# The second norm's blocks turned by VectorE behind a trip through DRAM, instead of by TensorE

## The reference

```
mod = silu(c) @ wmod            # sa, ca, ga, sb, cb, gb
h = layernorm(x) * (1 + ca) + sa
x = x + ga * (h @ (weight * blockmask).T + bias)        # 1024 x 1024, mask by 32 x 32 blocks
h = layernorm(x) * (1 + cb) + sb
x = x + gb * ((silu(h @ gate_w.T * gate_s) * (h @ up_w.T * up_s)) @ down_w.T * down_s)   # 2752 wide
```

## Time and profile before

| | us |
|---|---|
| median of 3 runs (lowest, highest) | 1110.01 (1108.84, 1110.47) |
| profiled execution | 1110.46 |
| its span, first to last instruction | 1108.7 |
| TensorE busy | 1080.1 |
| VectorE busy | 739.0 |
| ScalarE busy | 428.1 |
| GpSimd busy | 376.4 |

### The profile page before, as it was taken

The page is one execution under the profiler, slowest core; times in us unless marked ns, Lnnn a source line. Parts: engine busy times, 40 slices in busy tenths (PEclk is TensorE's granted clock), DMA queues, the critical chain, the costliest instruction groups (busy, mean ns, idle before and its releaser), DMA issues. The chain is left out here.

```text
span 1108.7 us, 13305 instructions
## 1 busy us (share of the span) xinstructions
PE 1080.1 (97%) x4753; PEld 501.3 (45%) x4753; DVE 739.0 (67%) x939; ACT 428.1 (39%) x783; POOL 376.4 (34%) x348
## 2 busy tenths in 40 slices
PE   5999999999999999999999999999999999999998
PEld 3443444545444444444444444444444444444444
DVE  4448478766688998889797888879545434334434
ACT  2322157556564554446555555555432000000000
POOL 2115446647644442326455555655200000000000
PEclk9999999999999999999999999999999999999999
DMA  9994223235453655445666666665298666566430
GB/s 345 388 388 114 80 72 95 68 103 162 143 194 129 169 174 171 129 125 166 195 205 180 184 191 184 186 203 180 74 353 330 246 251 235 223 240 235 194 127 38
DMA packets 132049, 206.94 MB, mean 187 GB/s; under 512 B 20624, under 2 KB 99216, under 8 KB 129552
## 3 DMA queue, kind: packets, MB, share of 16 engines
q1 hardware_dynamic: 126688, 184.08, 50.4%
q0 software_dynamic: 5296, 22.02, 5.6%
HBM read 137.39 MB, written 68.68 MB: 186 GB/s over the span
## 5 line engine op out<-in xcount | busy, mean ns | idle before, releaser
L1436 PE MATMUL pA<-work 128*128 128x512 f16 x1680 | 377.0, 379 | 5.1 <-ACT work L1097 3.3
L1436 PEld LDWEIGHTS pA<-work 128*128 128x128 f16 x1680 | 163.8, 98 | 205.4 <-ACT work L1097 6.4
L1236 PE MATMUL pA<-work 128*128 128x512 f32 x512 | 227.3, 595 | 2.5 <-DVE work L1696 0.9
L1436 PE MATMUL pB<-work 128*128 128x512 f16 x752 | 175.9, 379 | 1.4 <-DVE work L1855 1.4
L1236 PEld LDWEIGHTS pA<-work 128*128 128x128 f32 x512 | 94.3, 190 | 112.9 <-issue 109.9
L1877 DVE SCALAR_TENSOR_TENSOR work<-work 128x512 f16<-128x512 f16 x144 | 122.7, 874 | 19.6 <-ACT work L1117 19.3
L1503 PE MATMUL pA<-work 128*128 128x512 f16 x600 | 134.4, 379 | 0.0
L1097 ACT ACTIVATE work<-pA 128x512 f32<-128x512 f32 x126 | 74.6, 592 | 116.3 <-PE pA L1436 111.0
L1436 PEld LDWEIGHTS pB<-work 128*128 128x128 f16 x752 | 73.5, 98 | 90.2 <-DVE work L1855 2.1
L946 ACT ACTIVATE work<-pB,small 128x128 f32<-128x128 f32 x240 | 86.8, 478 | 70.6 <-PE pB L1209 59.3
L1503 PE MATMUL pB<-work 128*128 128x512 f16 x480 | 107.5, 379 | 0.9 <-DMA work<-h_left_scratch 0.9
(11 more groups left out here) (178 smaller groups left out, 1058.9 us busy)
## 6 DMA issues: line engine op xcount, KB each, us to landing
work<-h_scratch SPq DMA_DIRECT2D x8, 4480.0 KB, 13.7
h_scratch<-work SPq DMA_DIRECT2D x60, 512.0 KB, 3.1
work<-in_L_wmod SPq DMA_DIRECT2D x10, 2048.0 KB, 16.6
work<-in_L_ffn_gate_w SPq DMA_DIRECT2D x84, 128.0 KB, 3.2
work<-in_L_ffn_up_w SPq DMA_DIRECT2D x84, 128.0 KB, 2.9
work<-down_scratch SPq DMA_DIRECT2D x7, 1280.0 KB, 11.5
work<-in_L_ffn_down_w SPq DMA_DIRECT2D x68, 128.0 KB, 2.8
work<-in_L_attn_data SPq DMA_DIRECT2D x16, 512.0 KB, 4.2
```

The source lines that it names most:

```text
L1236: last = pe.matmul(pA[:, 2 * par(t) + h, :], hT1[par(t)][:, c, :], wT[:, c, h * H:(h + 1) * H], start=(c == 0), stop=(c == KT - 1))
L1436: last = pe.matmul(ps, w[:, m, c], bc[b][:, mv_, s, c], start=begin, stop=(i == n - 1 and c == KT // 2 - 1 and s == 1), skip_group_check=True)
```

## The change

The second norm's blocks are no longer turned by TensorE. `normalise(1, t)` writes `z2` in its own order of columns, SyncE stores it to a scratch in DRAM (`store_z`) and loads it back in four loads arranged like those of the weights (`load_zb`) into `zb`, which shares its place with a row used before and after. VectorE then turns it in one instruction into `z2T` in PSUM (`turn`), from where ScalarE goes on as before. There is one `zb`: `load_zb(t)` waits for the store of block t and for `turn(t - 1)`; `normalise(1, t)` waits for the store of block t-1.

The lists change with it. In VectorE's step t the first norm of block t+2 comes directly behind its statistics, ahead of the `lo_part`s; `turn` stands at the step's start (tables `FIRST` and steps 10 on) or behind `residual` (`SECOND`). The first two residuals are taken apart into scaling and finishing, and the second norm of block 0 goes behind `residual(2)`. On TensorE `gate_row(2)` stands ahead of the products of block 2 and the row sums 4 and 5 one place earlier, with `copy_row(5)` ahead of `evacuate(1)` on ScalarE. A mask quarter has one counter for its two loads in place of two. A wait of GpSimd for its own earlier root is added. The core of the diff:

```
+    z_v = z_d.rearrange("n (b j) (a k) -> n a j b k", b=A, a=A)
-        m_loaded = [sem(f"m_loaded{k}") for k in range(8)]
+        m_loaded = [sem(f"m_loaded{q}") for q in range(4)]
-        MID = {3: 0, 6: 1, 7: 3, 8: 5, 9: 6, **{t: t - 2 for t in range(10, NT + 1)}}
-        END = {6: 2, 7: 4, 9: 7}
+        zb = gbs
+        FIRST = {6: 1, 7: 3, 8: 5, 9: 6}
+        SECOND = {6: 2, 7: 4, 9: 7}
...
+            def store_z(t):
+                sp.wait_ge(z_done[1], t + 1)
+                sp.dma_start(z_d[t], z2).then_inc(z_stored, 16)
+            def load_zb(t):
+                sp.wait_ge(z_stored, 16 * (t + 1))
+                if t == 0:
+                    sp.wait_ge(acc_used, 2)
+                else:
+                    sp.wait_ge(t_done[1], t)
+                for a in range(A):
+                    sp.dma_start(zb[Q * a:Q * (a + 1)].rearrange("p (b k) -> p b k", b=A), z_v[t, a])\
+                      .then_inc(zb_loaded, 16)
...
+                if t in (3, 4):
+                    store_z(t - 3)
+                if t == 4:
+                    load_zb(0)
+                if t == 5:
+                    store_z(2)
+                    load_zb(1)
+                if t in FIRST:
+                    store_z(FIRST[t] + 2)
+                    load_zb(FIRST[t] + 1)
+                if t >= 10:
+                    store_z(t - 1)
+                    load_zb(t - 1)
+                if t in SECOND:
+                    if t < 9:
+                        store_z(SECOND[t] + 2)
+                    load_zb(SECOND[t] + 1)
...
+            row_sum(4)
             attend(1, 1, range(4, 6))
-            row_sum(4)
+            row_sum(5)
             attend(1, 1, range(6, KT))
-            row_sum(5)
+            gate_row(2, rowp[0])
...
-                if t in MID:
-                    transpose(1, MID[t])
-                if t in END:
-                    transpose(1, END[t])
-                if g == 1:
-                    transpose(1, LAST)
...
+            def turn(t):
+                dve.wait_ge(zb_loaded, 16 * A * (t + 1))
                 if t >= 1:
+                    dve.wait_ge(hf_ready, t)
+                else:
+                    dve.wait_ge(row_copied, 10)
+                dst = z2T.rearrange("p h n -> p (h n)")
+                dve.transpose(dst.rearrange("p (c b i) -> p c b i", c=KT, b=A),
+                              zb.rearrange("p (b c i) -> p c b i", b=A, c=KT)).then_inc(t_done[1], 1)
...
             def mask_quarter(q):
                 g, half = quarter(4 * q)
+                dve.wait_ge(m_loaded[q], 32)
                 for i in range(2):
-                    dve.wait_ge(m_loaded[2 * q + i], 16)
...
             for t in range(6, NT + 1):
+                if t in FIRST:
+                    turn(FIRST[t])
+                if t >= 10:
+                    turn(t - 2)
                 if t <= LAST - 2:
                     stats1(t + 2)
+                    normalise(0, t + 2)
+                if t in (7, 8, 9):
+                    lo_part(2 * t - 13)
                 if t in (6, 7, 8):
                     lo_part(2 * t - 12)
...
-                if t <= LAST - 2:
-                    normalise(0, t + 2)
-                if t in MID and t > 3 and t <= LAST:
-                    normalise(1, MID[t] + 1)
+                if t in FIRST:
+                    normalise(1, FIRST[t] + 2)
+                if 10 <= t <= LAST:
+                    normalise(1, t - 1)
                 if t <= LAST:
                     residual(t)
-                if t in END:
-                    normalise(1, END[t] + 1)
-                if t in (6, 7, 8):
-                    lo_part(2 * t - 11)
+                if t in SECOND:
+                    turn(SECOND[t])
+                    if t < 9:
+                        normalise(1, SECOND[t] + 2)
```

More of the change, by code:

```diff
@@ L1059, in _ @@
             copy_row(4)
+            copy_row(5)
             evacuate(1)
-            copy_row(5)
             for t in range(2, NT + 1):
@@ L1306, in _ @@
             pe.wait_ge(consts_set, NCONST)
-            transpose(0, 0)
+            transpose(0)
             pe.wait_ge(silu_c_done, 1)
@@ L1388, in _ @@
                     pe.wait_ge(bma_copied, 1)
-                if t == 2:
-                    attend(t, 0, range(4))
-                    gate_row(2, rowp[0])
-                    attend(t, 0, range(4, KT))
-                elif t <= LAST:
+                if t <= LAST:
                     attend(t, 0)
@@ L1808, in _ @@
             gate_a()
-            residual_of_evacuated(0)
+            scale_evacuated(0)
+            scale_evacuated(1)
+            finish(0)
+            finish(1)
+            stats1(4)
+            normalise(0, 4)
+            residual(2)
             normalise(1, 0)
-            residual_of_evacuated(1)
-            stats1(4)
+            stats1(5)
+            normalise(0, 5)
+            residual(3)
             dve.wait_ge(scales_loaded, 16 * 2 * (A + 1))
@@ L1815, in _ @@
             bound_of(3, sus)
-            normalise(0, 4)
-            residual(2)
-            stats1(5)
-            normalise(0, 5)
-            normalise(1, 1)
-            residual(3)
             stats1(6)
             normalise(0, 6)
+            normalise(1, 1)
             residual(4)
@@ L1829, in _ @@
             scales()
+            turn(0)
+            normalise(1, 2)
             residual(5)
             for t in range(6, NT + 1):
+                if t in FIRST:
+                    turn(FIRST[t])
+                if t >= 10:
+                    turn(t - 2)
                 if t <= LAST - 2:
                     stats1(t + 2)
+                    normalise(0, t + 2)
+                if t in (7, 8, 9):
+                    lo_part(2 * t - 13)
                 if t in (6, 7, 8):
@@ L1925, in _ @@
                 if g == 1:
+                    turn(LAST)
                     lo_part(LAST - 1)
```

39 lines of the change are left out of this document (20 added, 19 removed).

## The result

The changed kernel takes 1151.47 us (median of 4 runs, 1149.88 to 1151.80) against 1109.74 for the kernel before on the same chip: a ratio of 1.0371, 95% interval 1.0357 to 1.0384. It is slower by 41.7 us, where 1124, slower by 13.7, was forecast with a range up to 1136. The direction was right, the size was not. The profiled run has a span of 1149.7.

What follows compares the result with a forecast made beforehand. TensorE, busy 97%, was taken to bound the kernel before the change. Gone 18.3 us, come 32.0 (1.1 mask, 24.8 turn_out waits, 6.1 feed-forward start), net +13.7 on 1110.46: 1124, range 1110 to 1136.

Steps and rivals of the forecast that it cites:

- TensorE's list: On TensorE, all 16 turns of the second norm go, 14.0 us less, and the wait of 1.67 for z2 too.
- gate row: Moved ahead of block 2's products on TensorE: the waits of 0.79 and 0.47 go, together 1.3 us less.
- mask: One wait for both halves of a mask quarter: quarter 2's sums start later, +1.1 us, between 0 and 1.2.
- The place of the loss: TensorE waits for ScalarE's turn_out: 2.2, 7.0, 2.8, 9.0, 1.0, 2.8 us at blocks 8, 9, 11, 12, 13, 15; together 24.8.
- The trip: From z2 through DRAM to zb: 5.0 us queued behind the next store, 7.6 awaiting its own; bounds 3.9 and 5.7, 7 and 10.
- VectorE's rows: Durations laid end to end on VectorE: norm 0.8, even lo_part 1.2, odd 2.9 to 3.1, residual 4.0, turn 1.22 us.
- rival (c): GpSimd's sharing stretches each of ten steps by 1 us, with a half-speed stretch after a long wait: 1135, chance 0.20.
- The trips of blocks 11 and 13: In steps 11 to 15, each trip through DRAM takes 7.6 us, from above 10 when x1 stores and unit loads come between.
- The start of the feed-forward stage: Late hi_part(13) costs TensorE 1.6 us, unit 6 landing 4.5 late makes snap2 2.3 and up2_ready 2.2 late; together 6.1.
- The clock: Slow TensorE products after long waits: at most 6.9 us more per wait; none taken, 0 to 7 kept in the range.
- (a): TensorE stays the bound and the trip is hidden: -17 us, 1093, or 1109 with half the waits left; chance 0.12.
- (b): The shorter trips, 3.9 and 5.7 us, hold; waits shrink to about 15, net +3 to +5: 1114, chance 0.22.

Runs made afterwards that it cites:

- experiment 10: The kernel before with only one edit of the change, one wait for both halves of a mask quarter: 1111.17 us against 1110.08.
- experiment 1: The changed kernel with 30, 60, 66 and 44 useless TensorE products ahead of blocks 8, 9, 12 and 15: 1154.18 us.
- experiment 2: The changed kernel with 20, 40, 44 and 28 useless TensorE products ahead of blocks 8, 9, 12 and 15: 1153.63 us.
- experiment 4: The changed kernel, still one buffer, with ScalarE's list reordered so turn_out stands ahead of the second_input and cast before it: 1153.52 us.
- experiment 7: The changed kernel with units 6 and 7 loaded ahead of block 15's store and loads on SyncE: 1146.32 us.
- experiment 9: The changed kernel with GpSimd's two stores of the combos cut to a seventh of their bytes: 1146.63 us.
- experiment 6: The changed kernel, one buffer, with a block's loads ahead of the next block's store on SyncE in steps 5 to 9: 1129.06 us.

## Why the prediction was right in direction and wrong in size

**TensorE's list, gate row, mask: right.** The turns are gone. The row sums at 84.84 and the transposes at 106.01 wait for nothing, where 0.79 and 0.47 stood in the earlier trace rows; block 5's products end 0.9 sooner (144.64 for 145.57), by the terms 1.0. The mask wait, taken as 1.1, is 1.1 in experiment 10.

**The place of the loss: right.** ScalarE's list behind `second_input`, that behind VectorE's turn, that behind the trip; the longest waits at blocks 9 and 12, none at block 14. Block 10 waited 2.0 where none was forecast, and block 13 not at all.

**The trip: the first step that failed.** "0.5 + 1.3 + 3.2 = 5.0 if they only queue behind the next block's store." From the norm in front to the turn it was 5.9, 6.0, 7.8, 5.5 and 7.2 for `turn(1)` to `turn(5)`, two of them above the upper bound of 7. For the longest: the last load was issued 3.0 behind the norm (1.8 taken), and the turn started 4.8 behind that (3.2 taken). The prices were read where loads go alone. In the three shorter trips only the 512 KB store of the next block stood ahead of the loads, which made them 0.5 to 1.0 too long. In the two long ones GpSimd's store of the new `x` had begun 0.6 to 0.8 ahead of that store (170.27 and 171.09, 198.45 and 199.09): 2.2 to 2.8 too long. All six traces with this order of SyncE's list (the changed kernel, experiments 1, 2, 4, 7 and 9) part in the same way, 5.4 to 6.0 from store to turn against 7.1 to 8.0. `turn(8)`, with no store ahead of its loads but one of GpSimd's beside them (237.94), came 6.4 behind `turn(7)`, where 4.4 was laid out. The prediction kept these stores of `x` for its upper bound. No run moves them by themselves, so this parting is read from rows. The load of `x` that follows in both long trips is not it: it follows in experiment 6 too (168.90), where the loads landed in 2.9. The trip that waits for its own store was priced right: 7.1 to 7.8 for 7.6 at blocks 9, 10, 12 and 14.

**VectorE's rows: the second.** `turn(4)` ended 53.4 behind block 5's products where 43.6 was forecast. Of these 9.8 the four trips up to it make 5.1 and slow rows of VectorE 4.8: `lo_part(0)` and the norm of block 3 took 2.29 and 1.75 where 1.2 and 0.8 were taken, `lo_part(1)` 6.1 for 3.1. The prediction took the fast rows, though the means in the earlier trace rows were 1.70 and 1.03. The slow ones ran beside GpSimd's `sums`, here beside `lo_part(1)`:

```profile
183.18 1.30 POOL L850 TENSOR_TENSOR work<-work 128x512 f32<-128x512 f32 x1 [0.67 <-ACT work L984]
184.56 2.12 POOL L852 TENSOR_TENSOR work<-work 128x512 f32<-128x512 f32 x1
186.76 2.13 POOL L854 TENSOR_TENSOR work<-work 128x512 f32<-128x512 f32 x1
```

`lo_part(2)`, at 189.36 while GpSimd stood idle, took 1.21. That is the mechanism of rival (c), which had 1 us a step for it, where steps 6 and 7 show 4.8 in two. These rows agree with the rule of the Trainium skill (GPSIMD Engine Reference, Key points) weighed there. No experiment takes this part alone. At block 12, 17.4 late, the trips up to `turn(8)` make 11.6.

Experiment 6 shows what the first step weighs: with the loads ahead of the store, and nothing else changed, 22.4 of the 41.7 come back. Starts in us from the end of block 5's products (144.64 in the changed kernel, 144.29 in experiment 6):

| | forecast | changed kernel | experiment 6 |
|---|---|---|---|
| block 9 starts (turn_out(9) done) | 53.0 | 62.6 | 52.0 |
| block 12 starts | 108.6 | 126.0 | 107.4 |
| block 15 starts | 156.2 | 179.8 | 159.2 |
| waits for turn_out | 24.8 | 39.1 | 21.1 |
| time | 1124 | 1151.5 | 1129.1 |

That its starts come so near to the forecast's is in part luck. Up to `turn(4)` its trips are 4.2 shorter than forecast, since the loads no longer wait for the next block's norm, while its norms (twice 1.75), an even `lo_part` (2.29) and a wait for GpSimd's root (2.1) make VectorE 3.5 longer. The run prices the order; it does not show that the layout of the forecast holds.

A delay of 2 to 3 in a trip counts more than once, since with one buffer each load waits for the turn before it.

**The trips of blocks 11 and 13: outside the bounds.** 13.4 and 11.7 from store to turn, with 10 as the highest bound. The prediction named stores of x1 and loads of units as the neighbours; the 1.79 MB of combos that GpSimd stores in that moment it did not see. With these stores cut, in experiment 9, the two trips took 7.9 and 7.6, as laid out for such a trip, and the median is 4.8 lower. From block 12 to block 15 the kernel loses another 6.2 on the forecast.

**The start of the feed-forward stage: right to 1.5.** 1.6, 2.3 and 2.2 forecast; 3.3, 3.0 and 1.3 measured, at the places named, and `turn_unit(6)` waits 3.5 for its load (4.5 forecast).

**The clock: 0 taken, and nothing speaks against it.** The products behind the waits were slow, by 9.1 us at the four block starts shown and by 1.6 at the row of 362.41. The granted clock was 0.87 to 0.91 in the mean from 160 to 280 us, and 0.50, the 1.2 GHz level, right behind the waits. These rows agree with the rule of the Trainium skill (TensorE: Matmul & The Clock Gate, What's actually happening), and experiment 2 shows that idling is the reason. But where the fill took the slowness away, the time did not fall.

**The rivals.** (a) asked that the trips be hidden: with two buffers and the order mended it happens, and then the kernel is faster, but by 4 us and not 17. (b) asked for trips shorter than 5.0; they were longer. (c) had a mechanism that is in the rows, at about half of what block 9 was late, and 1135 for it, short of 1151.

## What to carry to other kernels

A transfer's price holds for the place in its queue from which it was read: loads behind one store of 512 KB came up to 1 us later here, and with a second store from another queue 2 to 3, so look at which store of any queue starts in the same moment. When a trip through DRAM goes through one buffer, its delay returns with every block; ordering the load ahead of the next store gave back 22 of 42 us here, and a second buffer with such an order 25. Before reordering the engine that is named in a wait, see what it waited for itself: ScalarE was named, VectorE's loop was late.

## What was not expected of the hardware

- Four loads of 128 KB landed 2.9 to 3.0 behind their issue with no other transfer near (experiment 6), 3.3 to 3.8 behind a 512 KB store in the same queue, and 4.6 where GpSimd's queue had begun a 512 KB store too. The four issues took 1.7 to 2.0, 2.2, and 2.6 to 2.9. Behind a 512 KB load of `x` and beside GpSimd's store it was 5.8 to 5.9 (experiment 6, at 156 and 210 us, where no turn waited for them).
- A 512 KB store of SyncE landed in 2.6 to 3.0 in the changed kernel where none of GpSimd's stood beside it; in 4.6 to 4.9 beside a 512 KB store from GpSimd's queue, and in 6.8 to 6.9 beside one of 1.79 MB.
- Beside GpSimd's `sums`, VectorE's `lo_part` instruction of 128x1024 took 2.29 for 1.22, and its norm 1.75 for 0.81.
- The stream transpose of VectorE into PSUM from a reloaded block takes 1.26, as long as one in SBUF (1.22).
- The same norm took 0.81 or 1.85 at the same place in two kernels that are alike up to there; a shift of 3 us at block 15 therefore need not come from an edit.
